# Other orders of work in an adaLN attention and quantised FFN kernel, with part of the FFN moved from VectorE to GpSimd

## The chip, the cores and the metric

The kernel runs on one core of one Trainium2 chip. The metric is device time in microseconds, the median of several executions; lower is better. Five engines work side by side and wait for each other by semaphores: TensorE (PE, with its weight loads as PEld), VectorE (DVE), ScalarE (ACT), GpSimd (POOL) and SyncE (SP), which here only issues DMAs. ScalarE issues the other DMAs.

## The reference, cut to what matters

`x` is (8, 256, 128). One layer is computed and added to `x`:

```python
# attention: 16 heads of 64, one shared key/value head, one extra "null" key
xn = ln(x, g_norm)
q = (xn @ Wq).reshape(b, n, 16, 64);  k, v = split(xn @ Wkv)
q = l2norm(q) * q_scale;  k = l2norm(k) * k_scale
sim = 8.0 * q @ k.T + attn_bias            # bias: a small MLP over relative positions
attn = softmax(causal(sim))
y = ln((attn @ v) @ Wout, g_out)
# FFN with fake quantisation to 8 bits; every scale is a maximum over the WHOLE tensor
xq = act_quant(y, clip_x)                  # scale = sigmoid(clip) * max|y| / 127
h = act_quant(silu(xq @ qw(w_gate).T) * (xq @ qw(w_up).T), clip_down)
return x + h @ qw(w_down).T
```

Two global maxima (of `y`, and of `h`) separate the kernel into stages: nothing of the FFN can start before the last `y`, and nothing can be rounded in the FFN's second half before the last `h`.

## The kernel before, in words

**Opening.** The relative-position MLP (`mlp_centre`, `mlp_silu`, `mlp_turn`), the keys of batch 0 (`k_norm2`, `k_normalise`, `kT_make`) and the first four "quarters" of q (`q_make_first`, `q_norm2`, `q_normalise`, `qT_make`, `qT_evac`) are made. A quarter is 128 rows by 8 heads. SP loads `b1b` and `g1b` (the MLP's second bias and gain) as its sixth and seventh DMA, lines 337 and 338.

**Loop.** `over_groups` runs every engine's `group(s)` over groups of four heads: `at` = 0 to 33, batch `s.b = at // 4`, `s.g = at % 4`. Each engine has its own hand-written order for a group; the engines are coupled by semaphores only. For a group, TensorE makes scores into two pairs of PSUM banks (front: heads 0 and 1, back: heads 2 and 3), the DVE adds the bias and takes row maxima (`score_pair`, L1227), ACT takes the exponent (`exponent`, L576), the DVE inverts the row sums (`invert`, L1235), POOL multiplies by the inverses (`normalise`, L443), TensorE transposes (`turn`, L917), ACT copies the result out (`pT_evac`, L586). One group later TensorE multiplies by the values (`values`, L874), the DVE copies that out (`oT_copy`, L1217) and TensorE multiplies by `Wout` (`y_products`, L829). The same loop carries the work of the next batches: x statistics (`x_stats`, `x_power`, `x_normalise`), keys (`kv_make`, `kv_evac`, `k_norm2`, `k_power`, `k_normalise`, `kT_make`) and one quarter of q per group (`q_make`, `q_square`, `q_norm2`, `q_power`, `q_normalise`). POOL's square roots are powers with exponent -0.5 (L396).

**Last groups.** Groups 32 and 33 hold no new scores (`s.live` is false). TensorE leaves them to `flush()`: it turns group 31's heads 0 and 1, multiplies the values of group 30, turns heads 2 and 3, and so on. Heads are turned only when ACT has emptied the pT buffer by reading order, since pT has one set of four tiles.

**FFN.** `ffn()` on TensorE; k counts 512-row blocks (4), f counts 128-wide tiles of the hidden width (IT = 3). ACT makes silu of the gate product (L662), the DVE multiplies it by the up product straight from PSUM (L1381). For f = 2 instead ACT copies both to SBUF (L671, L673) and POOL multiplies them (L474). The DVE takes one maximum per tile (`h_absmax`, L1360). After the second global maximum the DVE rounds to int8 (`h_quantise`, L1396), ACT widens to bf16 (L679), TensorE makes the down product, the DVE scales it (`down_scale`, L1400) and adds x (L1404, L1421), POOL adds x for block 1 (L477), SP stores.

## Time and profile before

| what | us |
|---|---|
| median of 3 executions | 302.04 (300.73 to 302.70) |
| the profiled execution | 302.66 |
| its span, first to last instruction | 300.9 |
| busy: PE, DVE, ACT, POOL | 259.3, 237.3, 228.0, 204.0 |

The profiled execution is 0.6 us above the median, and 1.8 us of it lie outside the span. Times in the rows below are microseconds from the start of the span. In a row of a timeline the first number is the start, the second the length, and "xN" merges N neighbouring instructions of one line. "idle before" is how long the engine had nothing to do and who ended that. In the loop a batch takes 29.05 us.

### The profile page before, as it was taken

To read this page: it belongs to the slowest core of one execution; us is meant where nothing else is said; L and a number is where in the kernel's file an instruction comes from. 1 tells how busy PE (TensorE), PEld (TensorE's weight loads), DVE (VectorE), ACT (ScalarE), POOL (GpSimd) and SP (SyncE) were. 2 spreads that over 40 slices of the span, in tenths; PEclk is the share of its full clock that TensorE was granted. 3 is DMA by queue.
4 is the path that set the end of the run, shared out by engine and by line. 5 is a ranking of instruction groups with operands and counts; after the bars stand their busy time and mean duration, and the time that the engine had idled before them with its cause. 6 is when DMAs were issued, how large, how long until landed. Compare 5 with 4: busy or idle time off the path is not lost.

```text
span 300.9 us, 7310 instructions
## 1 busy us (share of the span) xinstructions
PE 259.3 (86%) x2161; PEld 204.1 (68%) x2162; DVE 237.3 (79%) x965; ACT 228.0 (76%) x785; POOL 204.0 (68%) x394
## 2 busy tenths in 40 slices
PE   0769899989999999999999999999999987875260
PEld 0427778877787888778788878888787865761050
DVE  2758887887888888879887988787876767559993
ACT  1555989978987888888789978998888877249480
POOL 2277888788788779878987898778877755013301
PEclk9989999999999999999999999999999999899756
DMA  4279000000000000000000000000000020000013
GB/s 140 49 183 268 2 1 2 1 3 2 1 2 1 3 1 2 0 3 1 2 0 4 3 0 2 0 4 0 2 2 3 2 72 1 2 0 1 0 36 110
DMA packets 13083, 6.89 MB, mean 23 GB/s; under 512 B 1953, under 2 KB 12913, under 8 KB 13042
## 3 DMA queue, kind: packets, MB, share of 16 engines
q1 hardware_dynamic: 11874, 6.03, 7.5%
q10 hardware_dynamic: 1168, 0.36, 0.5%
q8 instruction: 20, 0.33, 0.5%
q14 instruction: 21, 0.17, 0.2%
HBM read 5.31 MB, written 1.07 MB: 21 GB/s over the span
## 4 chain that ended last, share of the span: by engine, by line
PE 63%; DVE 16%; POOL 5%; ACT 5%; issue 4%; DMA 3%; SPq 1%; POOLq 0%; DVEq 0%; ACTq 0%
PE bank L874 13%; PE bank L829 10%; PE front L855 7%; PE back L917 7%; PE front L917 5%; PE bank L718 5%; PE back L855 5%; PE bank L734 4%; DMA g1b<-in_L_cond_g_dram 3%; ACT prob L576 2%; DVE score L1227 2%; POOL prob L443 2%; DVE hmax L1360 2%; DVE oT L1217 2%; DVE oT L1396 2%
## 5 line engine op out<-in xcount | busy, mean ns | idle before, releaser
L576 ACT ACTIVATE prob<-score,negmax 128x258 f32<-128x258 f32 (+1 forms) x256 | 113.5, 450 | 30.5 <-DVE negmax L1227 30.5
L443 POOL TENSOR_SCALAR prob<-prob,rrow 128x258 f32<-128x258 f32 x254 | 107.3, 441 | 23.0 <-DVE rrow L1235 19.7
L396 POOL TENSOR_TENSOR rq<-qn,neghalf 128x8 f32<-128x8 f32 x32 | 53.3, 1666 | 2.7
L874 PE MATMUL bank<-pT,val 128*64 128x256 f32 (+1 forms) x512 | 49.7, 337 | 0.6 <-ACT pT L586 0.6
L576 ACT ACTIVATION_READ_ACCUMULATOR prob<-score,negmax 128x1 f32 x256 | 49.1, 192 | 0.0
L874 PEld LDWEIGHTS bank<-pT,val 128*64 128x64 f32 x512 | 32.2, 138 | 20.7 <-ACT pT L586 10.7
L829 PE MATMUL bank<-wout,oT 128*128 128x128 f32 x256 | 36.8, 287 | 5.4 <-DVE oT L1217 4.7
L1227 DVE CUSTOM_DVE_ANT_0 score<-back,bias 128x258 f32<-128x258 f32 (+1 forms) x128 | 38.0, 353 | 0.1
L1227 DVE CUSTOM_DVE_ANT_0 score<-front,bias 128x258 f32<-128x258 f32 (+1 forms) x128 | 37.8, 351 | 0.0
L829 PEld LDWEIGHTS bank<-wout,oT 128*128 128x128 f32 x256 | 31.0, 191 | 10.0 <-DVE oT L1217 6.9
L1096 DVE TENSOR_REDUCE qn<-sq 128x8 f32<-128x512 f32 x32 | 21.9, 685 | 19.6 <-ACT sq L522 19.0
L586 ACT COPY pT<-back 128x384 f32<-128x384 f32 x64 | 29.4, 480 | 4.7 <-PE back L917 3.4
L917 PE MATMUL back<-ident,prob 128*128 128x128 f32 x192 | 31.6, 285 | 0.1
L917 PE MATMUL front<-ident,prob 128*128 128x128 f32 x192 | 29.7, 273 | 1.1 <-POOL prob L443 1.1
L855 PE MATMUL front<-kT,qT 64*128 64x258 f32 (+1 forms) x256 | 29.7, 350 | 0.6 <-DVE qT L1107 0.2
L1217 DVE COPY oT<-bank 128x512 f32<-128x512 f32 x32 | 22.0, 688 | 9.0 <-PE bank L874 7.2
L586 ACT COPY pT<-front 128x384 f32<-128x384 f32 x64 | 26.7, 466 | 2.3 <-PE bank L874 2.3
L855 PEld LDWEIGHTS front<-kT,qT 64*128 64x128 f32 x256 | 22.2, 186 | 7.9 <-issue 5.4
L855 PE MATMUL back<-kT,qT 64*128 64x258 f32 (+1 forms) x256 | 26.9, 328 | 0.0
L917 PEld LDWEIGHTS back<-ident,prob 128*128 128x128 f32 x192 | 21.7, 144 | 5.1 <-DVE negmax L1227 3.4
L917 PEld LDWEIGHTS front<-ident,prob 128*128 128x128 f32 x192 | 22.8, 141 | 1.5 <-ACT pT L586 1.5
L855 PEld LDWEIGHTS back<-kT,qT 64*128 64x128 f32 x256 | 22.2, 187 | 2.2 <-issue 0.7
(199 smaller groups left out, 458.3 us busy)
## 6 DMA issues: line engine op xcount, KB each, us to landing
bias<-relative_table SPq DMA_DIRECT2D x8, 256.0 KB, 5.0
out_dram<-prob SPq DMA_DIRECT2D x4, 256.0 KB, 3.1
X<-in_x_dram SPq DMA_DIRECT2D x1, 896.0 KB, 13.3
prob<-in_L_cond_Wq_dram SPq DMA_DIRECT2D x1, 512.0 KB, 5.9
wout<-in_L_cond_Wout_dram SPq DMA_DIRECT2D x1, 512.0 KB, 14.5
prob<-in_L_ffn_w_down_dram SPq DMA_DIRECT2D x1, 176.0 KB, 2.4
X<-in_x_dram SPq DMA_DIRECT2D x1, 128.0 KB, 4.1
prob<-in_L_ffn_w_gate_dram SPq DMA_DIRECT2D x1, 128.0 KB, 2.1
```

Source lines behind the costliest of these rows:

```text
L396: pool.tensor_tensor(dst, src, neghalf[:, 0:width], ALU.pow).then_inc(done, 1)
L443: pool.tensor_scalar(prob[:, par, h, cols], prob[:, par, h, cols], rrow[:, par, h, t:t + 1], 1.0, ALU.mult, ALU.mult).then_inc(normed, 1)
L576: act.activation(prob[:, par, h, cols], score[:, h % 4, cols], ACT.Exp, scale=-1.0, bias=negmax[:, par, h, t:t + 1], accum_out=rowsum[:, p ...
L586: act.copy(pT[:, h % 4, :], bank[i][:, 0:3 * P]).then_inc(pT_ready, 1)
L718: last = pe.matmul(ps[:, :], xx[par][:, P * (q % 2):P * (q % 2) + P], ww[:, 512 * (q // 2):512 * (q // 2) + 512], start=xx is xTh and ww i ...
L829: pe.matmul(y_out(t), oT[:, m % 2, k, t * P:t * P + P], wout[:, k, :], start=k + t == 0, stop=False, skip_group_check=True)
L855: product = pe.matmul(banks[a][:, at:at + KEYS1 - c0], qT[par][rows, h // 2, t * P:t * P + P], kT[par][rows, c0:KEYS1], start=not masked, ...
L874: last = pe.matmul(ps[a * D:a * D + D, pair * N + i0:pair * N + N], val[m % 2][:, blk, :], pT[:, 2 * pair + a, c0:c1], start=blk == 1, sto ...
L917: product = pe.transpose(bank[i][:, k * P:k * P + P], prob[:, par, h, c0:c0 + P], ident[:, :])
L1096: dve.tensor_reduce(qn2[:, q, :], sq[:, :, :], AX.X, ALU.add).then_inc(q_n2, 1)
L1217: dve.tensor_copy(oT[:, m % 2, 2 * g:2 * g + 2, :].rearrange("p k n -> p (k n)"), (q_ps if at == GB * B - 1 else val_ps)[:, :])\
L1227: dve.tensor_tensor_reduce(score[:, h % 4, c0:c0 + w], ps[:, c0:c0 + w], bias[:, h, 0:w], -1.0, -3.0 * NEG, ALU.add, ALU.min, negmax[:, pa ...
```

## The change

1. **FFN.** `POOLED` names five (k, f) tiles instead of the four of f = 2: (0,2), (1,1), (1,2), (2,2), (3,2). The DVE makes seven products instead of eight. The twelve maxima become eight instructions, four of which cover two tiles. Block 0's addition of x goes from the DVE to POOL, and so does the multiplication that makes `sds`. All twelve `h_quantise` roundings come ahead of the first `down_scale`. The last maximum before the FFN takes one instruction less behind `yraw`.
2. **Loop.** On the DVE `invert` of the previous group's heads 2 and 3 moves behind the first `score_pair`, `k_normalise` moves from ahead of `oT_copy` to behind that `invert`, `k_norm2` goes ahead of `x_normalise`, `x_stats` one group earlier (g = 2). On POOL `x_power` moves from g = 0 of a batch, between two `normalise`, to g = 3 of the batch before, ahead of `q_power`. On ACT `kv_evac` goes between the two pairs of `pT_evac`.
3. **Last groups.** The loop ends at `LOOP = 30`; groups 30, 31 and the flush are written out in `ending()`. TensorE makes group 31's products in another order; group 30's turned heads are copied out by the DVE into a buffer of their own, `pTe`, so that ACT's copies of group 31 need not wait for `values(30)`; the weight preparation of the FFN (`ffn_weights`) is spread differently.
4. **Opening.** `b1b` and `g1b` are issued by ACT, ahead of `condk`, `qs` and `ks`. TensorE gets 40 idle transposes at the start and 3 in each `mlp_turn`, 6 more ahead of `qT_make(0)` and 6 ahead of the reading of the mask's minimum. `q_make_first(2)` goes ahead of the MLP's second layer. On the DVE the mask's minimum (L1142) moves from the start to behind `q_normalise(0)`, the table behind `k_normalise(0)`; `q_normalise(2)` goes between group 0's score pairs and `x_normalise(1)` behind them.

```diff
+POOLED = [(0, 2), (1, 1), (1, 2), (2, 2), (3, 2)]
+OWN = [(k, f) for k in range(4) for f in range(IT) if (k, f) not in POOLED]
+LOOP = GB * B - 2
...
 # POOL, group()
+                if s.g == 3 and s.b + 3 < B:
+                    x_power(s.b + 3)
                 if s.quarter is not None and s.quarter >= 4:
                     q_power(s.quarter, s.quarter % 4)
...
-                if s.g == 0 and s.prev is not None and s.b + 2 < B:
-                    x_power(s.b + 2)
...
+            def ending():
+                y_power(B - 2)
+                normalise(heads(LOOP - 1)[2:4])
+                for at in (LOOP, LOOP + 1):
+                    normalise(heads(at)[0:2])
+                    normalise(heads(at)[2:4] if at == LOOP else heads(at)[2:3])
+                y_power(B - 1)
...
 # PE
             pe.wait_ge(consts, 3)
+            keep_busy(40, qT_ps)
...
+            def ending(masked):
+                s = Group(LOOP)
+                first_scores(s, masked)
+                pe.wait_ge(pT_ready, GH * (LOOP - 1))
+                second_scores(s, masked)
+                values(LOOP - 2)
+                turn(s, 0)
+                turn(s, 1)
+                for pair in range(2):
+                    y_products(LOOP - 2, pair)
+                turn(s, 2)
+                turn(s, 3)
+                s = Group(LOOP + 1)
+                first_scores(s, masked)
+                pe.wait_ge(pT_ready, GH * LOOP)
+                second_scores(s, masked)
+                turn(s, 0)
+                turn(s, 1)
+                values(LOOP - 1)
+                turn(s, 2)
+                turn(s, 3)
+                for pair in range(2):
+                    y_products(LOOP - 1, pair)
+                s = Group(GB * B)
+                for i in range(4):
+                    turn(s, i)
+                pe.wait_ge(yT_ready, B - 1)
+                null_weights(s.null)
+                values(LOOP)
+                values(LOOP + 1)
+                for at in (LOOP, LOOP + 1):
+                    for pair in range(2):
+                        y_products(at, pair)
+                y_null(s.null)
...
 # DVE, group()
-                if s.kT is not None:
-                    k_normalise(s.kT)
...
                 if s.summed is not None:
                     oT_copy(s.summed)
                 if s.g == 2 and s.prev is not None:
                     y_normalise(s.prev)
-                if s.turned is not None and s.live:
+                if s.first:
+                    dve.wait_ge(ld_bias[s.g], 16 * 2)
+                score_pair(heads(s.at)[0:2])
+                if s.turned is not None:
                     invert(heads(s.turned)[2:4])
+                if s.kT is not None:
+                    k_normalise(s.kT)
+                if s.quarter >= 4:
+                    q_normalise(s.quarter, s.quarter % 4, q_ps)
+                if s.at == 0:
+                    q_normalise(2, 2, q_ps0[2])
+                score_pair(heads(s.at)[2:4])
+                if s.at == 0:
+                    x_normalise(1)
+                    qT_evac(2, 2, 0)
+                    q_normalise(3, 3, q_ps0[3])
+                invert(heads(s.at)[0:2])
...
 # DVE, the last groups
+            def pTe_copy(i):
+                dve.wait_ge(pT_done, heads(LOOP)[i][0] + 1)
+                dve.tensor_copy(pTe[:, i, :], bank[i][:, 0:3 * P]).then_inc(pTe_ready, 1)
...
 # DVE, FFN
+            h_product(0, 0)
+            h_product(0, 1)
+            h_absmax(0, 0, 0, 2)
+            h_product(1, 0)
+            h_absmax(1, 0, 2, 1)
+            h_absmax(2, 1, 0, 1)
+            h_product(2, 0)
+            h_product(2, 1)
+            h_absmax(3, 1, 1, 2)
+            h_absmax(4, 2, 0, 2)
+            h_product(3, 0)
+            h_product(3, 1)
+            h_absmax(5, 2, 2, 1)
+            h_absmax(6, 3, 0, 2)
+            h_absmax(7, 3, 2, 1)
...
+            for k in range(4):
+                h_quantise(k)
+            dve.wait_ge(sds_ready, 1)
+            for k in range(3):
+                down_scale(k)
```

## Rows read from the trace of the kernel before

**Rows 1.** Page: the span and its instructions.

```profile
span 300.9 us, 7310 instructions
```

**Rows 2.** Windows: length, then busy us of PE, PEld, DVE, ACT, POOL, then clock.

```profile
37.00:239.20 202.20, 197.95 (x1749) 161.82 (x1750) 168.08 (x742) 173.06 (x638) 165.36 (x319) 1.00 0.01 2
...
239.20:263.60 24.40, 21.05 (x175) 16.41 (x175) 15.70 (x66) 14.66 (x56) 9.88 (x25) 0.93 0.08 24
```

**Rows 3.** Waits, 38 to 239.3: us in total, times, longest.

```profile
PE bank L829 <- DVE oT L1217: 3.9, 6, 0.8
```

**Rows 4.** Timeline of POOL, DVE and PE, 116 to 122 (a group with g = 1).

```profile
116.89 1.80 POOL L443 TENSOR_SCALAR prob<-prob,rrow 128x258 f32<-128x258 f32 x4
...
119.09 0.72 POOL L396 TENSOR_TENSOR rk<-kn,neghalf 128x2 f32<-128x2 f32 x1
...
120.39 0.68 DVE L1217 COPY oT<-bank 128x512 f32<-128x512 f32 x1
...
121.12 1.16 PE L829 MATMUL bank<-wout,oT 128*128 128x128 f32 x8 [0.72 <-DVE oT L1217]
```

**Rows 5.** Timeline of DVE and POOL, 99 to 103 (a group with g = 2).

```profile
99.08 0.17 DVE L1235 RECIPROCAL rrow<-rowsum 128x4 f32<-128x4 f32 x1
...
99.16 0.40 DVE L1227 CUSTOM_DVE_ANT_0 score<-front,bias 128x258 f32<-128x258 f32 x1
...
100.11 1.66 POOL L443 TENSOR_SCALAR prob<-prob,rrow 128x258 f32<-128x258 f32 x4
...
100.25 0.69 DVE L1102 TENSOR_TENSOR qn<-bank,rq 128x512 f32<-128x512 f32 x1
...
102.35 1.66 POOL L443 TENSOR_SCALAR prob<-prob,rrow 128x258 f32<-128x258 f32 x4 [0.57 <-DVE rrow L1235]
```

**Rows 6.** Chain of waits of the opening: start, us, what.

```profile
3.43 10.39 DMA g1b<-in_L_cond_g_dram
...
37.05 0.94 PE bank L718 x3
```

**Rows 7.** Landing of ks, from its issue at 3.94.

```profile
L486 ACTq DMA_DIRECT2D ks<-in_L_cond_k_scale_dram x1: 453/453/453, 3.9 to 3.9; - x1
...
DMA to landing us min/median/max: 11.2/11.2/11.2
```

**Rows 8.** Timeline of DVE, group 0.

```profile
28.34 0.42 DVE L1227 CUSTOM_DVE_ANT_0 score<-front,bias 128x258 f32<-128x258 f32 x1
...
31.96 0.17 DVE L1235 RECIPROCAL rrow<-rowsum 128x4 f32<-128x4 f32 x1
```

**Rows 9.** Windows as in Rows 2, around two falls of the clock.

```profile
17.00:20.00 3.00, 1.04 (x4) 0.31 (x4) 1.25 (x5) 2.44 (x5) 2.54 (x3) 0.94 0.88 211
...
20.00:23.00 3.00, 2.85 (x8) 1.74 (x9) 1.20 (x3) 0.99 (x6) 2.07 (x3) 0.50 0.25 64
...
255.20:258.60 3.40, 3.40 (x23) 2.48 (x19) 1.23 (x3) 1.21 (x3) 0.11 (x1) 0.50 0.02 5
```

**Rows 10.** Chain of waits of the last groups.

```profile
254.79 2.50 PE bank L874 x16
...
257.29 1.45 PE back L917 x6
...
263.63 0.51 DVE ost L1241 x2
```

**Rows 11.** Timeline of DVE, ACT and POOL, FFN.

```profile
271.60 0.75 DVE L1381 SCALAR_TENSOR_TENSOR prob<-back,sgu,oT 128x512 f32<-128x512 f32 x1
...
273.62 1.28 ACT L662 ACTIVATE oT<-front,sgu 128x512 f32<-128x512 f32 x2
...
281.87 2.45 DVE L1360 TENSOR_REDUCE hmax<-prob 128x1 f32<-128x512 f32 x4
...
293.48 1.26 DVE L1404 TENSOR_TENSOR prob<-prob,X 128x512 f32<-128x512 f32 x1
...
295.57 0.69 DVE L1421 TENSOR_TENSOR prob<-prob,X 128x512 f32<-128x512 f32 x1
```

More of the change, by code:

```diff
@@ L97, in held @@
     eng.sem_inc(passed, 1)
+LOOP = GB * B - 2
 def over_groups(group):
-    for at in range(GB * B + 2):
+    for at in range(LOOP):
         group(Group(at))
@@ L206, in build @@
         ymax = sb("ymax", [P, B])
+        gabs = sb("gabs", [P, 1])
         yraw = sb("yraw", [P, 1])
@@ L336, in _ @@
             sp.dma_start(mask_u[:, :], mask.rearrange("(a b) n -> a (b n)", a=1)).then_inc(ld_mask, 16)
-            for dst, src in ((b1b[:, :], row(b1)), (g1b[:, :], row(g1))):
-                sp.dma_start(dst, src).then_inc(ld_mlp, 16)
             for dst, src in ((w2s[:, :], w2), (b2c[:, :], col(b2))):
@@ L484, in _ @@
             act.dma_start(w1s[:, :], w1).then_inc(ld_w1, 16)
+            for dst, src in ((b1b[:, :], row(b1)), (g1b[:, :], row(g1))):
+                act.dma_start(dst, src).then_inc(ld_mlp, 16)
             for dst, src in ((condk[:, :], row(cond[0])), (qs[:, :], row(q_scale)), (ks[:, :], row(k_scale))):
@@ L542, in _ @@
             mlp_turned(0)
+            kv_evac(0, halves(misc))
+            q_square(0, q_ps0[0])
+            q_square(1, q_ps0[1])
+            mlp_silu(1)
+            mlp_turned(1)
+            q_square(2, q_ps0[2])
+            act.wait_ge(kT_done, 1)
+            for par in range(2):
+                act.copy(kT[par][:, 0:KEYS1:P + 1], misc[:, 2 * P:2 * P + 2]).then_inc(null_a, 1)
+            kT_evac(0, halves(misc))
+            v_copy(0)
+            act.activation(table_load[:, 1:2], neghalf[:, 0:1], ACT.Exp)
+            q_square(3, q_ps0[3])
+            act.wait_ge(wq_ready, 1)
+            act.copy(wqh[:, :], wq[:, :]).then_inc(wq_high, 1)
             act.wait_ge(ld_mask, 16)
@@ L616, in group @@
                     pT_evac(s.turned, 1)
-                if s.at == GB * B - 1:
-                    exponent(heads(s.at)[3])
+                if s.kv is not None:
+                    kv_evac(s.kv, front_tails)
                 if s.turned is not None:
@@ L623, in group @@
                     null_evac(s.null)
-                if s.kv is not None:
-                    kv_evac(s.kv, front_tails)
                 if s.kT is not None:
@@ L735, in qT_make, with keep_busy @@
                 last.then_inc(qT_done, 1)
+            def keep_busy(count, ps):
+                for _ in range(count):
+                    pe.transpose(ps[:, 0:P], ident[:, :], ident[:, :])
             def mlp_turn(layer):
@@ L742, in mlp_turn @@
                 last.then_inc(mlp_t, 1)
+                keep_busy(3, qT_ps)
                 pe.wait_ge(mlp_a, 2 * layer + 2)
-            def keep_busy(count, ps):
-                for _ in range(count):
-                    pe.transpose(ps[:, 0:P], ident[:, :], ident[:, :])
             pe.wait_ge(consts, 3)
+            keep_busy(40, qT_ps)
             for t in range(2):
@@ L867, in values @@
                 last_group = at == GB * B - 1
+                turned = pTe if at == LOOP else pT
                 ps = q_ps if last_group else val_ps
@@ L874, in values @@
                             last = pe.matmul(ps[a * D:a * D + D, pair * N + i0:pair * N + N], val[m % 2][:, blk, :],
-                                             pT[:, 2 * pair + a, c0:c1], start=blk == 1, stop=blk == 0,
+                                             turned[:, 2 * pair + a, c0:c1], start=blk == 1, stop=blk == 0,
                                              skip_group_check=True)
@@ L1179, in _ @@
             q_norm2(3, 3)
-            q_normalise(2, 2, q_ps0[2])
-            x_normalise(1)
             def ffn_weights(h):
@@ L1274, in group @@
             def group(s):
-                if s.quarter is not None and s.quarter >= 4:
+                if s.quarter >= 4:
                     q_norm2(s.quarter, s.quarter % 4)
-                if s.kT is not None:
-                    k_normalise(s.kT)
-                if s.turned == GB * B - 1:
-                    invert(heads(s.turned)[2:4])
-                    last_normalise()
                 if s.summed is not None:
```

286 lines of the change are left out of this document (142 added, 144 removed).

## The prediction, made blind

> **What bounds the kernel now.** I read the page first, for the span of 300.9 us [rows 1], then the windows by stage. The reader is to see there that the loop is TensorE's: from 37 to 239.2 it is busy 197.95 of 202.2 us at full clock, while the next engine, ACT, has 173.06 [rows 2]. So a change of order in the loop can give back about 4 us at most, which is what PE lacks. The waits say where those are: 3.9 us in six waits of `y_products` on the copy `oT` [rows 3], one in each g = 1 group of batches 1 to 6. The last groups are another thing: 24.4 us, in which PE is busy 21.05 us, part of it at half clock [rows 2]. The FFN's first half is the DVE's, without a gap worth naming between 271.60 and 284.3 [rows 11]. The opening hangs on a DMA and then on a chain that goes through all engines [rows 6].
>
> **Loop, the wait that goes.** In g = 1 POOL normalises from 116.89 to 118.69, then makes `rk` until 119.81; the DVE scales the keys after it and only then copies `oT`, from 120.39; `y_products` starts at 121.12, 0.72 us late [rows 4]. Afterwards `oT_copy` comes first, and stands behind nothing but `values`, which ends near 118.9. With 0.7 us for the copy [rows 4] it is there by 119.7, before PE has made its scores (it would ask at 120.4). `x_power` is gone from ahead of that `normalise`, so the keys are scaled near 121.5, behind the first score pair, and are wanted at about 121.8. All six waits go: -3.9 us. If the keys come late, the wait returns there, at the 0.3 us or so that I have misjudged. `kv_evac` fills a pause of ACT before the back pair is turned; `x_stats` and `x_power` in their new places fill pauses of over 1 us that their engines had while q was squared. I count these at nothing; without the pause each costs its own length of up to 1 us, once a batch.
>
> **Loop, the wait that comes.** `invert` of heads 2 and 3 now stands behind four score halves. In g = 2 it ran at 99.08, the halves took 99.16 to 100.25, that is 1.09 us, and POOL began with those heads at 100.11, as soon as it was free [rows 5]. POOL starts 0.38 us after an `invert` starts (101.97 to 102.35, the release in the last line of [rows 5]). The new `invert` starts at 100.17, so POOL starts at 100.55, 0.44 late, and ends at 102.21 instead of 101.77 (1.66 us for four instructions [rows 5]). Head 3 is turned today once its scores are taken from PSUM, at 102.05, so 0.16 us of the 0.44 shows. Six batches: +1.0 us. In the other groups POOL is held by the powers of q until after the new `invert`. Loop: -2.9 us, bounds -3.9 (the lag hides) and -1.2 (all of 0.44 shows in six groups).
>
> **Last groups.** Today this stage is a zigzag: values of group 30 wait for ACT's last exponents and copies, and PE idles and falls to half clock. The values at 254.79 take 2.50 us for 16 products against the loop's 1.45, the turns at 257.29 take 1.45 against 0.66 [rows 10]; the clock row beside them is 0.50 [rows 9]. That excess is 1.05 + 0.8 = 1.85 us. At full clock PE's work here is 21.05 - 1.85 = 19.2 us. In the new order I walked through the queues from 239.2 on. Three waits remain on PE: 0.75 us ahead of `y_products(28)`, because the DVE takes two score pairs (2 x 1.09 us [rows 5]) before `oT` and `yn`; 0.7 us ahead of `y_products(29)`, whose copy (0.68 [rows 4]) stands behind two `pTe` copies; 0.5 us for POOL's head 2 of group 31. So y is complete at 239.2 + 19.2 + 1.95 = 260.35 by busy times. Walking by starting times, which overlap less in the count, gives 259.1. Today it is 263.63 [rows 10]. That is -3.3 to -4.5; I take -4.0. Behind it `gabs`, one maximum and the joined end lie beside POOL's power of about 1.2 us; one small DVE instruction goes from the path, -0.25 us.
>
> **FFN, first half.** The DVE goes from 8 to 7 products (0.66 us apart), -0.66 us; a maximum costs 0.6 (2.45 us for four [rows 11]), of which about 0.06 is not streaming, and four joined pairs save 0.25. From this the DVE would need 11.6 instead of 12.7 us. But each tile given to POOL costs ACT two passes instead of one. ACT's passes are 0.58 us apart (two of them end 1.15 us after 273.62 [rows 11]). After 273.62 ACT has one pass for (1,0), two for (1,1), the widening of xq (0.51), two for (1,2), then (2,0), which starts at 273.62 + 5 x 0.575 + 0.51 = 277.0. The DVE product follows a gate by 0.74 us, so at 277.7; the DVE has by then done its three products and maxima up to block 1 and is idle since 276.4. That wait of 1.3 us, with 0.4 us of smaller ones for (1,0) and (0,2), more than eats the 0.9 us. From 277.7 on: 4 products, 2.64, 7 tiles of maxima, 3.9 with joins, and the gap to the end gives 285.0 with the last reduction, against 284.3: +0.7 us. Bounds: -0.9, if ACT does not hold it, and +1.0.
>
> **FFN, second half.** With all roundings first ACT loses its wait of 0.3 us, but the third down product waits for `down_scale(0)`, which comes after twelve roundings. The DVE's last addition starts at 295.57 [rows 11]; I come to 295.5. I take -0.05, bounds -0.6 and +0.4. In the row of 293.48 the addition takes 1.26 us, against 0.69 for the same shape at 295.57 [rows 11], and POOL's addition runs beside it. The Trainium skill (SBUF — State Buffer, section "SBUF: two separate sides") says that the DVE and GpSimd share one pair of ports under an exclusive lock, and the loser waits. By that rule two additions on POOL would hold the DVE's until the second ends, and the last addition would start at 295.65, which moves the sum by 0.1.
>
> **Opening.** `g1b` lands 10.39 us after its issue, at 13.82 [rows 6]. Ahead of three loads on ACT's queue it should land near 11.5, so the MLP's second layer starts at about 12, 1.9 us sooner. But the `ks` load moves behind it. It lands at 15.1 today [rows 7], when nobody waits; now the DVE will stand at it from about 13.3, and every power on POOL is queued behind. I take 15.5 for it (bounds 14 and 17.5). From there the chain of powers and q quarters brings the first scores of group 0 to the DVE at 25.6 if TensorE is at full clock, at 26.7 if it is at half, against 28.34 [rows 8]. Then the order in group 0 takes some back. From first score to `invert` it is 3.62 us today (28.34 to 31.96 [rows 8]); with `q_normalise(2)` between the pairs, and `x_normalise(1)` behind them, for which PE's x transposes and so its q transposes wait, I add up 5.5 us. `q_make(4)` is due at 36.9 (half) or 35.8 (full) instead of 37.05 [rows 6]: -0.15 or -1.2 us. I take -0.7, bounds +1.3 (ks at 17.5) and -2.0. The 40 transposes lie ahead of the first x and cover nothing; at the slow spacing they would end at 10 and cost up to 0.3.
>
> The clock decides between those two. Its row is 0.50 for 20 to 23, after a stretch of 3 us in which PE worked 1.04 us [rows 9], and the new opening leaves PE about as sparse there. By the Trainium skill (TensorE: Matmul & The Clock Gate, "What's actually happening") the low rate is the default and comes back after an idle window. By that rule alone the opening, which has no long idle stretch, would keep full clock and give -1.2; the row shows that a stretch that is not idle was enough for the fall.
>
> **Sum.** -0.7 - 2.9 - 4.0 - 0.25 + 0.7 - 0.05 = -7.2 us. The profiled execution took 302.66 and becomes 295.5; it stands 0.6 above the median, so from 302.04 I get 294.8.
>
> **Rivals.** *The fall of the clock stays in the last groups*: PE still has 1.95 us of waits there, and one fall costs the 1.85 us above: 296.7. *The FFN is not held by ACT*: -0.9 instead of +0.7: 293.2. *Keys late*: ks at 17.5 or later, opening +1.3 instead of -0.7: 296.8. *Full clock from the transposes on*, the skill's rule named above: 294.3. *The cuts of waits do nothing*, as POOL's and DVE's chain through q bounds a group at the same 7.0 us anyway and the six waits only move to the turns: loop 0, 297.7. *The other side*: the later `invert` puts POOL on the path in every one of 29 groups. Each then loses the 0.44 us, 12.8 us in place of the 1.0 that I count: 306.6. Against it: in g = 0 and 3 POOL is bound by the powers of q, which end after the new `invert`. It would decide from 0.25 us a group on (7.2 / 29).
>
> **How the numbers follow.** Forecast 0.45, clock rival 0.15, FFN rival 0.1, keys 0.1, full clock 0.06, waits only moved 0.1, POOL in every group 0.04. The range takes in all but the last, with the bounds that add up at the low side: 291.0 to 299.0. About 1% is what a measurement of this kernel can tell from no change, so faster means below 299.0: 0.89. Within 1%: 0.07, where two of the rivals fall together. Slower: 0.04.
>
> **What would show it.** Right: no wait of `y_products` on `oT` in the loop and a batch of about 28.5 us instead of 29.05; a wait of some 0.15 us more in the turn of head 3 in g = 2; 19 to 21 us from the scores of group 30 to `y_stats(7)` with the clock at 1.00; a DVE gap of about 1.3 us ahead of product (2,0); in the opening a DVE wait for the `ks` load. Wrong: gaps of PE in front of each turn of head 2 (POOL in every group); a first `invert` after 33; a clock row of 0.50 in the last groups.

## The result, and the profile after

| | before | changed |
|---|---|---|
| median of 20 executions each, us | 301.84 (299.51 to 304.01) | 302.61 (301.04 to 305.75) |
| the profiled execution, us | 302.66 | 301.27 |

The ratio on record is 1.0055, 95% interval 1.0031 to 1.0079: no gain at all, where 294.8 us and a gain of 7 us had been forecast. (It isn't the quotient of the two medians, which is 1.0026; the loss is 0.8 us by the medians and 1.7 by the ratio.) Six of the changed kernel's 20 executions, two of them counted as slow and left out of the ratio, took 304.3 to 305.8 us at a mean granted clock of 0.946 to 0.948, where the others have 0.959 to 0.975; none of them was traced, so what happens there stays open. The changed kernel's profiled execution lies 1.3 us below its own median, that of before 0.8 us above its own, so the pair of traces shows a span 1.5 us shorter where the medians show 0.8 us longer. The traces are used here for where the time goes inside, and the medians for what a version is worth.

The page of the changed kernel, its span:

```profile
span 299.4 us, 7421 instructions
```

I put the same events of the two traces side by side (start times from the timelines, us) and subtracted from one mark to the next. "Forecast" is the term of the prediction's sum:

```
event                                    before   changed  later by   stage: measured  forecast
q_make(4), PE                             37.05    39.97    +2.92     opening  +2.92    -0.7
front scores of group 30, PE             239.21   242.44    +3.23     loop     +0.31    -2.9
y_stats(7), DVE                          263.63   262.96    -0.67     last gr. -3.90    -4.0
first product of the FFN, DVE            271.60   270.73    -0.87              -0.20    -0.25
second global maximum (amax), DVE        284.36   284.23    -0.13     FFN 1    +0.74    +0.7
last addition of x, DVE                  295.57   295.18    -0.39     FFN 2    -0.26    -0.05
end of the span                          300.85   299.40    -1.45     store    -1.06     none
```

Four terms came out close to the forecast; two, the opening and the loop, are wrong by 3.6 and 3.2 us, together 6.8 of the forecast gain of 7.2. The last line isn't an effect of the change: from the last addition to the end took 5.28 us in before, 4.22 here, and between 4.17 and 5.58 in the other kernels below, all with the same last store.

**Loop.** Windows: length, then busy us of PE, PEld, DVE, ACT, POOL, then clock. The same stretch, from the first scores of group 2 to those of group 30, of the changed kernel and then of before; the last row is the changed kernel's last groups, to be read against [rows 2]:

```profile
40.84:242.44 201.60, 197.45 (x1747) 161.31 (x1747) 166.66 (x736) 175.67 (x634) 165.18 (x316) 1.00 0.01 2
```

```profile
37.91:239.21 201.30, 197.08 (x1747) 161.35 (x1747) 167.32 (x736) 172.16 (x635) 164.46 (x317) 1.00 0.01 2
```

```profile
242.40:262.90 20.50, 18.77 (x175) 15.33 (x176) 16.66 (x69) 13.19 (x52) 9.78 (x25) 1.00 0.11 28
```

TensorE lacks 4.15 us in the changed loop and 4.22 in the old one. So its waits haven't gone, although the waits of [rows 3] have: the waits of PE in the changed loop, 40 to 242.4 us, in total, times and longest, are these, and none is on `oT`:

```profile
PE back L964 <- POOL prob L452: 1.7, 6, 0.3
PE front L738 <- DVE kz L1150: 0.6, 1, 0.6
PE back L857 <- POOL prob L452: 0.5, 2, 0.3
PE bank L755 <- issue: 0.5, 1, 0.5
PE bank L773 <- DVE qn L1167: 0.4, 1, 0.4
```

The time itself shows the rest of the account. The lag behind before at the front scores of a group, us:

```
group   2     3     4     5     6     7     8     9     10    11   ...  26    27    28    29    30
lag   +2.92 +3.45 +4.29 +4.58 +3.84 +4.09 +4.10 +4.13 +3.48 +3.73 ... +2.58 +2.82 +3.04 +3.23 +3.23
```

Each batch gains 0.64 to 0.74 us where the wait on `oT` stood (group 5 to 6, 9 to 10 and so on; only 0.14 in batch 6), 3.4 us in all. Each then loses 0.25 between g = 2 and g = 3. But ahead of that, between group 2 and group 5, stands a loss of 1.66 us that comes once, and that no step of the prediction had.

**The g = 2 group.** Timeline of the DVE, POOL and PE, 101 to 106 us: start, length, engine, line, and in brackets the idle time ahead and who ended it.

```profile
103.68 0.17 DVE L1298 RECIPROCAL rrow<-rowsum 128x4 f32<-128x4 f32 x1
...
104.07 3.07 POOL L452 TENSOR_SCALAR prob<-prob,rrow 128x258 f32<-128x258 f32 x7 [0.44 <-DVE rrow L1298]
...
105.88 0.52 PE L964 MATMUL back<-ident,prob 128*128 128x128 f32 x3 [0.29 <-POOL prob L452]
```

`invert` stands behind the first score pair, POOL is idle 0.44 us until it comes, and the turn of head 3 is 0.29 us late. The 0.44 is the number of the prediction to the digit; what PE sees of it was put at 0.16.

**The start of the loop.** Timeline of PE, DVE and POOL, 43 to 55 us (groups 2 and 3, batch 0):

```profile
43.26 0.69 DVE L1280 COPY oT<-bank 128x512 f32<-128x512 f32 x1 [1.00 <-PE bank L921]
...
45.07 0.58 DVE L1150 SCALAR_TENSOR_TENSOR kz<-kv,rk,qks 128x128 f32<-128x128 f32 x2
...
53.26 0.69 DVE L1167 TENSOR_TENSOR qn<-bank,rq 128x512 f32<-128x512 f32 x1 [0.80 <-POOL rq L409]
```

```profile
45.80 0.30 PE L738 MATMUL front<-ident,kz 128*128 128x128 f32 x1 [0.64 <-DVE kz L1150]
...
54.01 0.66 PE L773 MATMUL bank<-ident,qn 128*128 128x128 f32 x4 [0.39 <-DVE qn L1167]
```

```profile
50.43 0.71 POOL L409 TENSOR_TENSOR rstd<-mv,neghalf 128x2 f32<-128x2 f32 x1
```

The keys of batch 1 are scaled one group later than in the other batches (`late` is 1 in batch 0). At 42.26 the DVE had nothing to do for 1.00 us, which is where `k_normalise` stood; now it runs at 45.07, behind a score pair, and TensorE waits 0.64 us for it. One group on, `x_power(3)` (50.43, with its short instruction at 50.16) is ahead of `q_power`, so q is scaled at 53.26 after 0.80 us of idle DVE, and TensorE waits 0.39. These two waits, and one of 0.26 us on POOL at 62.54 (the first of L857), are 1.3 us of the 1.66; no wait of TensorE in the trace names the rest.

**Opening.** Timeline of ACT, 4.8 to 12.4 us:

```profile
4.84 0.45 ACTq L509 DMA_DIRECT2D ks<-in_L_cond_k_scale_dram  x1
5.33 5.61 ACTq L511 DMA_DIRECT2D vcol<-in_cond_dram  x2
...
12.37 0.68 ACT L552 ACTIVATE prob<-prob,mrs 128x128 f32<-128x128 f32 x2
```

ACT issues eleven loads now. The first nine take 0.45 to 0.68 us each, the last two together 5.61 us (1.21 and 4.37 by the chain of waits), and in that time ACT does nothing else: its first silu starts at 12.37 instead of 9.03. TensorE stands still for the last 3.79 us of the way there, and the granted clock falls behind that, from 14.1 to 17.5 us, and is at 1.00 from there into the FFN:

```profile
13.10 0.44 PE L785 MATMUL front<-ident,prob 128*128 128x128 f32 x2 [3.79 <-ACT prob L552]
```

The chain of waits that ends in the first score goes through the MLP's second layer, which comes behind the keys (its silu at 19.63), and through two instructions that the change had moved there, the table and the mask's minimum:

```profile
21.90 0.47 DVE table L1234
...
22.97 0.79 DVE mask_min L1237
```

Then the DVE in group 0 (timeline, 29 to 35 us), against [rows 8]:

```profile
29.08 0.43 DVE L1290 CUSTOM_DVE_ANT_0 score<-front,bias 128x258 f32<-128x258 f32 x1 [1.15 <-PE front L898]
...
30.20 0.69 DVE L1167 TENSOR_TENSOR qn<-bank,rq 128x512 f32<-128x512 f32 x1
...
31.92 0.85 DVE L1133 TENSOR_SCALAR xn<-X,mv,rstd 128x128 f32<-128x128 f32 x2
...
34.94 0.17 DVE L1298 RECIPROCAL rrow<-rowsum 128x4 f32<-128x4 f32 x1
```

and the wait of PE that belongs to it, in the waits of 28.5 to 40 us:

```profile
PE bank L724 <- DVE xn L1133: 2.8, 1, 2.8
```

TensorE stands 2.8 us in front of the transposes of `xn`, which the DVE makes only behind both score pairs of group 0. From first score to first `invert` it is 5.86 us, against 3.62. The first `invert` is at 34.94; the prediction had named one after 33 as a sign that it is wrong.

**Last groups and FFN.** The waits of PE, 242.4 to 263 us:

```profile
PE bank L872 <- DVE yn L1313: 1.1, 1, 1.1
PE back L964 <- POOL prob L452: 0.4, 1, 0.4
PE bank L747 <- DVE negmax L1290: 0.2, 1, 0.2
```

1.7 us of waits remain, and the clock is 1.00 throughout. That holds beyond this trace: the two traces with the old last groups have the fall of the clock in them and take 24.4 us from the front scores of group 30 to `y_stats(7)`, the eleven with the new ones have no fall there and take 20.5. In the FFN (timeline of ACT and the DVE, 274 to 285 us) the wait that was forecast is there:

```profile
276.13 1.32 ACT L702 ACTIVATE oT<-front,sgu 128x512 f32<-128x512 f32 x2
```

```profile
274.26 1.28 DVE L1452 TENSOR_REDUCE hmax<-prob 128x1 f32<-128x512 f32 x2
276.90 0.75 DVE L1470 SCALAR_TENSOR_TENSOR prob<-back,sgu,oT 128x512 f32<-128x512 f32 x1 [1.36 <-ACT oT L702]
```

### The profile page after: what moved, and what is told of

It is laid out like the page before. It is cut to its first block, busy times and chain, and to the rows that moved or that the text cites. A ratio compares the mean times of both kernels' runs of the same rounds, so it can differ in the third digit from the quotient of the medians.

```text
span 299.4 us, 7421 instructions
## 1 busy us (share of the span) xinstructions
PE 264.1 (88%) x2219; PEld 211.4 (71%) x2220; DVE 235.9 (79%) x963; ACT 229.9 (77%) x782; POOL 207.4 (69%) x397
## 4 chain that ended last, share of the span: by engine, by line
PE 60%; DVE 20%; POOL 7%; issue 6%; ACTq 3%; ACT 3%; DVEq 0%; POOLq 0%
PE bank L921 14%; PE front L898 7%; PE bank L872 7%; PE back L964 7%; PE bank L755 6%; POOL prob L452 5%; DVE score L1290 5%; PE back L898 4%; PE front L964 4%; PE bank L773 3%; DVE oT L1280 2%; ACTq L511 2%; DVE oT L1495 2%; DVE hmax L1452 2%; DVE yn L1313 1%
## 5 line engine op out<-in xcount | busy, mean ns | idle before, releaser
L599 ACT ACTIVATE prob<-score,negmax 128x258 f32<-128x258 f32 (+1 forms) x256 | 113.4, 450 | 16.4 <-DVE negmax L1290 16.4
L921 PE MATMUL bank<-pT,val 128*64 128x256 f32 x496 | 47.1, 332 | 0.0
L921 PEld LDWEIGHTS bank<-pT,val 128*64 128x64 f32 x496 | 30.8, 136 | 19.3 <-ACT pT L609 9.9
L609 ACT COPY pT<-back 128x384 f32<-128x384 f32 x62 | 28.7, 482 | 9.0 <-PE back L964 8.6
L964 PE MATMUL back<-ident,prob 128*128 128x128 f32 x192 | 30.2, 277 | 2.8 <-POOL prob L452 2.1
L898 PE MATMUL back<-kT,qT 64*128 64x258 f32 (+1 forms) x256 | 26.7, 326 | 0.0
```

The source lines that it names most:

```text
L599: act.activation(prob[:, par, h, cols], score[:, h % 4, cols], ACT.Exp, scale=-1.0, bias=negmax[:, par, h, t:t + 1], accum_out=rowsum[:, p ...
L609: act.copy(pT[:, h % 4, :], bank[i][:, 0:3 * P]).then_inc(pT_ready, 1)
L898: product = pe.matmul(banks[a][:, at:at + KEYS1 - c0], qT[par][rows, h // 2, t * P:t * P + P], kT[par][rows, c0:KEYS1], start=not masked, ...
L921: last = pe.matmul(ps[a * D:a * D + D, pair * N + i0:pair * N + N], val[m % 2][:, blk, :], turned[:, 2 * pair + a, c0:c1], start=blk == 1, ...
L964: product = pe.transpose(bank[i][:, k * P:k * P + P], prob[:, par, h, c0:c0 + P], ident[:, :])
```

## The experiments

Each version was timed with runs of the kernel before beside it, whose median was 301.20 us in the first four, 301.77 in the next four and 301.94 in the last three; it was 301.84 beside the changed kernel. Where two versions of different rounds are compared, the difference is taken of their distances to these medians, and the plain one is given too. "Stage" below is the difference between two of the marks of the table above.

**Theory:** the opening loses because ACT is held at its queue, because `x_normalise(1)` stands behind group 0's scores, and because `ks` is late; the loop loses because of the first batch and of `invert` in g = 2. **Main rival:** one cause only. If ACT's hold were all, its removal would give the opening back; if the order in group 0 were all, the hold would cost nothing.

### The vcol loads on SyncE

```diff
 # ACT
-            for dst, src in ((vcol[0:D, :], ...), (vcol[D:P, :], ...)):
-                act.dma_start(dst, src).then_inc(ld_v, 16)
 # SP, behind wout
+            for dst, src in ((vcol[0:D, :], ...), (vcol[D:P, :], ...)):
+                sp.dma_start(dst, src).then_inc(ld_v, 16)
```

> The changed kernel, but the two vcol loads are issued by SP behind wout instead of by ACT as its tenth and eleventh load. Theory 1 (ACT stood 4.4 us at the issue of its last load, and the MLP started 3.3 us late for that): ACT's first silu comes back to about 9 us from 12.37, the first scores of group 0 reach the DVE at 26 to 27 instead of 29.08, and group 1's first scores start about 2 us earlier than in the changed kernel (33.6). Time about 2 us below the changed kernel. Rival (the ks load and POOL's powers bound the opening anyway): silu early, but first scores still at 28.5 or later, time unchanged.

Measured: 303.59 us, ratio 1.0083 (1.0043 to 1.0123). The hold is gone, the silu starts at 8.97 instead of 12.37, and nothing is gained: the first score comes at 29.27, and the median is 2.4 us above that of before beside it, against 0.8 for the changed kernel. Timeline of the DVE in this kernel, 17 us:

```profile
17.22 0.23 DVE L1223 CUSTOM_DVE_ANT_0 ksq<-condk 128x64 f32<-128x64 f32 x1 [3.68 <-DMA ks<-in_L_cond_k_scale_dram]
```

The DVE stands 3.68 us at the load of `ks`. In the changed kernel it arrives at the same instruction at 17.30, when `ks` has landed (16.94). So up to this instruction the hold was hidden behind the late `ks`, to within 0.1 us. Behind it the two traces are not alike. TensorE has nothing to do for 5.16 us here; the clock is at 0.50 from 16.6 to 23.5 us (and again from 33.7 to 37.1), while the changed kernel has 1.00 from 17.5 on; and the idle transposes of the change (`keep_busy`, L780) stand in the chain of waits with 3.07 us. Timeline of PE, then three pieces of the chain:

```profile
19.51 0.69 PE L785 MATMUL front<-ident,prob 128*128 128x128 f32 x2 [5.16 <-ACT prob L552]
```

```profile
20.20 0.64 PE bank L780 x3
...
22.64 1.12 PE bank L780 x6
...
25.06 1.31 PE bank L780 x12
```

The run shows that taking the hold away alone brings nothing. It doesn't show that the hold is free at equal clock, and whether the chain would be shorter without these 21 transposes, of which 15 are the change's, was not run.

### x_normalise(1) back ahead of group 0's scores

```diff
             q_norm2(3, 3)
+            x_normalise(1)
...
                 if s.at == 0:
-                    x_normalise(1)
                     qT_evac(2, 2, 0)
```

> The changed kernel, but x_normalise(1) stands ahead of group 0's first score pair again, as before the change. Theory 1 (PE's x and q transposes wait for it): PE's wait of 2.75 us ahead of xT_make(1) goes, group 1's first scores start 1.5 to 2 us earlier than 33.6, the time falls by about 1.5 us. Rival (ACT's exponents bound group 0 and 1): the wait moves to the first invert, and group 2's first scores stay at 40.8.

Measured: 300.39 us, ratio 0.9950 (0.9915 to 0.9985). From first score to `invert` 4.04 us instead of 5.86; the wait of 2.8 us is gone; the lag at group 2 falls from 2.92 to 1.28 us. One moved pair of instructions is worth 1.6 us in the trace, and 1.6 in the medians as well (0.8 above before turns into 0.8 below; 2.2 from median to median).

### Both

The two edits above together.

> The changed kernel with both edits: vcol on SP and x_normalise(1) ahead of group 0's scores. If the two causes are independent, group 2's first scores start at about 37 (40.84 changed, 37.91 before) and the time is 3.5 to 4 us below the changed kernel, so about 299 against 301.8 before. If they share one bound, the gain is no more than the larger one, about 2 us.

Measured: 300.58 us, ratio 0.9962 (0.9932 to 0.9993), as with the second edit alone: again nothing is gained by taking away the hold. The trace is like that of the first run, with TensorE idle for 5.52 us, the clock at 0.50 from 18.4 to 25.2 us, and 3.23 us of idle transposes in the chain of waits.

### The opening of before

The changed kernel with the orders and loads of the old opening.

> The changed kernel with the whole opening as before (loads, idle transposes, orders of ACT, PE and DVE up to and in group 0), loop, last groups and FFN as changed. Theory 1: group 2's first scores start at 37.9 as before the change, the later transient of groups 2 to 5 and the rest stay, so the time is 2.9 us below the changed kernel. Rival (the opening's loss would be made up later in the loop, as POOL's and DVE's chain sets the pace): group 10 starts at the same time as in the changed kernel, 101.2, and the time is unchanged.

Measured: 299.83 us, ratio 0.9938 (0.9902 to 0.9974). The whole new opening costs 2.1 us by the medians (0.8 above before turns into 1.4 below; 2.8 from median to median), and 2.4 in the traces, where the lag at group 2 falls from 2.92 to 0.48. The lag rises from 0.48 at group 2 to 2.10 at group 5: the loss of 1.62 us at the loop's start is there with the old opening as well, so it belongs to the loop.

### The new last groups alone

The kernel before, with `ending()`, `LOOP` and the maximum that takes one instruction less behind `yraw`.

> The kernel before with the new last groups alone (opening, loop and FFN as before). Theory: the last groups were worth 3.9 us in the changed kernel and depend on nothing else that changed, so y_stats(7) starts 3.9 us earlier than in before (263.6 to 259.8) with no fall of the clock behind 240 us, and one DVE instruction less brings 0.2 more: 297.1 us beside 301.2. Rival: a good part of the 3.9 us came from the state in which the new loop leaves the engines, or the clock falls again: 299 us or more.

Measured: 298.43 us, ratio 0.9885 (0.9835 to 0.9936). Stage from the scores of group 30 to `y_stats(7)`: 3.9 us shorter than before, with no fall of the clock there. The median gains 3.3 us of the 4.1 that the stages show; the interval (296.8 to 299.8) holds both.

### The new FFN alone

> The kernel before with the new FFN alone (five tiles on GpSimd, joined maxima, all roundings first, two additions on GpSimd). Theory: the first half loses 0.74 us to the wait of the product (2,0) for ScalarE, the second gains 0.26: 301.7 us beside 301.2, with a VectorE gap of 1.4 us ahead of that product. Rival: the wait was due to the stages before, and the first half gains 0.9: 300.1 us.

Measured: 301.70 us, ratio 0.9994 (0.9963 to 1.0025). First half +0.73 us, second half -0.27. The wait for ACT has nothing to do with the stages before.

### The keys' loads on SyncE, ahead of x

On top of both opening edits:

```diff
 # SP, behind nb and ahead of the large load of x
+            for dst, src in ((condk[:, :], ...), (qs[:, :], ...), (ks[:, :], ...)):
+                sp.dma_start(dst, src).then_inc(ld_keys, 16)
             sp.dma_start(X[:, 2:, :], x_dram[:, 2:, :]).then_inc(ld_x, 16)
 # ACT: condk, qs, ks go, the two vcol loads come back
```

> The kernel with both opening edits (x_normalise(1) first, ScalarE's queue not full), and now condk, qs and ks issued by SyncE ahead of the large load of x, the two vcol loads back on ScalarE. Theory: in the last two runs with an early silu the chain hung on the landing of ks at 17.2 and 17.5; ahead of the load of x it lands near 14, and the first score comes at 26.5 instead of 29.9: 297.4 us. Rival: ks is late for the sake of the DMA engines, not of the queue, or TensorE runs at half clock in the gap: first score 28.5 or later, 299.5 us or more.

Measured: 298.17 us, ratio 0.9890 (0.9851 to 0.9929). Timeline of the DVE:

```profile
16.06 0.23 DVE L1223 CUSTOM_DVE_ANT_0 ksq<-condk 128x64 f32<-128x64 f32 x1 [1.35 <-DMA ks<-in_L_cond_k_scale_dram]
...
26.71 0.43 DVE L1291 CUSTOM_DVE_ANT_0 score<-front,bias 128x258 f32<-128x258 f32 x1 [0.15 <-DMA bias<-relative_table]
```

`ks` lands at 16.0 instead of 17.5: 1.5 us earlier, not the 3.5 that I expected of the queue's order. It takes 10.7 us from its issue in the new place and 12.1 in the changed kernel, so most of its lateness isn't the order on ACT's queue. The first score is 3.2 us earlier than in the kernel with both edits. 1.5 us of that is `ks`; the remaining 1.7 goes with the clock, which in the trace of that kernel is at 0.50 from 18.4 to 25.2 us and here at 1.00 from 14.5 us on. An early `ks` with ACT's hold left in place was not run. Now the load of the bias is what ends last.

### The loop repaired

On top of the old opening:

```diff
+                if s.kT is not None and s.first:
+                    k_normalise(s.kT)
                 if s.summed is not None:
                     oT_copy(s.summed)
...
+                if s.g == 2:
+                    invert(heads(s.turned)[2:4])
                 score_pair(heads(s.at)[0:2])
-                if s.turned is not None:
+                if s.turned is not None and s.g != 2:
                     invert(heads(s.turned)[2:4])
...
-                if s.g == 2 and s.b + 3 < B:
+                if s.g == (3 if s.first else 2) and s.b + 3 < B:
                     x_stats(s.b + 3)
 # POOL: x_power(3) back to group 4
```

> The changed kernel with the opening of before, and two repairs of the loop: in batch 0 k_normalise(1) is ahead of oT_copy, x_stats(3) and x_power(3) where they were before; in every g = 2 group invert of heads 2 and 3 is ahead of the first score pair again. Theory: the start-up loss of 1.6 us between group 2 and group 5 goes, and so does the 0.25 us a batch of g = 2 (1.5 us): 296.8 us beside 299.8 without the repairs. Rival for the first: the start-up loss comes from the kernel's state at that point and stays, 298.3 us. Rival for the second: PE's wait moves to the score copies behind the invert, and a batch stays as long as it was, also 298.3 us.

Measured: 296.22 us, ratio 0.9817 (0.9789 to 0.9845), 3.6 us below the same kernel without the two repairs (4.2 by the distances to before; the loop in the two traces is 2.7 us shorter, 198.75 against 201.47). Groups 2 to 5 take 22.78 us (before 22.73, changed 24.38), and g = 2 to g = 3 loses nothing in later batches. The waits of PE from 38 to 237 us, all of them:

```profile
PE back L851 <- POOL prob L454: 0.3, 1, 0.3
```

```profile
38.38:237.13 198.75, 197.52 (x1748) 161.29 (x1747) 166.93 (x736) 175.40 (x634) 163.98 (x316) 1.00 0.01 2
```

The loop takes 198.75 us, 2.55 less than before. Both rivals fall. The edit moves `k_normalise`, `x_stats` with `x_power`, and `invert` at once, so how the 1.66 us of the start divide between them isn't shown.

### Four tiles on GpSimd, joined maxima

```diff
-POOLED = [(0, 2), (1, 1), (1, 2), (2, 2), (3, 2)]
+POOLED = [(0, 2), (1, 2), (2, 2), (3, 2)]
...
             h_product(1, 0)
-            h_absmax(1, 0, 2, 1)
-            h_absmax(2, 1, 0, 1)
+            h_product(1, 1)
+            h_absmax(1, 0, 2, 1)
+            h_absmax(2, 1, 0, 2)
...
-            h_absmax(3, 1, 1, 2)
+            h_absmax(3, 1, 2, 1)
```

> The kernel with the opening of before and the repaired loop, with four tiles on GpSimd in the FFN as before (f = 2 of every block), but joined maxima and all roundings first. Theory: the fifth tile is what costs, as ScalarE needs two passes for it; the first half then takes 12.5 us from the first product to the second maximum instead of 13.5 (before 12.76), the second half keeps its gain of 0.26 us: 295.2 us beside 296.2 with five tiles. Rival: the joined maxima themselves cost (they wait for the later of two products) and the first half stays at 13.3 or more: 296.0 us.

Measured: 294.88 us, ratio 0.9753 (0.9706 to 0.9800). Timeline of the DVE, 269 to 278 us:

```profile
270.82 0.74 DVE L1467 SCALAR_TENSOR_TENSOR prob<-back,sgu,oT 128x512 f32<-128x512 f32 x1
...
277.60 0.16 DVE L1487 TENSOR_REDUCE amax<-hmax 128x1 f32<-128x8 f32 x1
```

No idle time ahead of any product, first half 12.58 us (five tiles 13.50, before 12.76). The joined maxima gave 0.18 us where 0.25 was forecast; the fifth tile cost 0.92.

### All that helped, together

> All that helped together: the new opening with x_normalise(1) first and the condk, qs and ks loads on SyncE, the repaired loop, the new last groups, four pooled tiles with joined maxima. Theory: the gains add, 298.2 - 1.6 (start-up) - 1.5 (g = 2) - 1.0 (FFN) = 294.1 us, with TensorE at full clock to the first scores. Rival: with the first scores 3 us earlier the loads of the bias (they ended last ahead of the first score in the run with the keys on SyncE) or the transient of batch 0 take back what the repair of the loop gave: 295.7 us.

Measured: 294.72 us, ratio 0.9761 (0.9713 to 0.9809). The better opening shows in the trace (q, scores and `y_stats(7)` all 1.5 us earlier than in the kernel before this one) but not in the medians of six and four executions. Whether it is worth anything in this combination stays open.

### Without the 40 idle transposes

> The kernel with all together, without the 40 idle transposes that TensorE makes ahead of its first transpose of x. Theory: they lie in a stretch in which TensorE waits for x anyway and cost nothing, and they keep the granted clock at 1.00 until the keys are made; without them a row of 0.50 appears before 20 us and the first score comes about 1 us later: 295.1 us. Rival: they make no difference to the clock, 294.1 us.

Measured: 293.53 us, ratio 0.9742 (0.9694 to 0.9789), against 0.9761 with them: no difference that these runs can tell. My theory of them falls all the same: no row of 0.50 appears before 20 us without them, and the first score comes 0.95 us earlier, at 25.72. The windows of the kernel with the transposes, and then of the one without (columns as above):

```profile
16.00:19.00 3.00, 1.61 (x10) 0.94 (x11) 1.66 (x5) 2.05 (x5) 2.83 (x5) 1.00 1.04 260
19.10:22.50 3.40, 3.40 (x14) 2.67 (x13) 3.40 (x6) 2.18 (x6) 2.27 (x4) 0.50 0.19 50
```

```profile
16.00:19.00 3.00, 1.85 (x10) 0.90 (x10) 1.62 (x5) 2.05 (x5) 2.83 (x5) 1.00 1.08 272
19.10:22.50 3.40, 3.37 (x25) 2.60 (x24) 3.40 (x6) 2.94 (x8) 2.27 (x4) 1.00 0.18 37
```

```profile
12.79 1.91 PE L725 MATMUL bank<-prob 128*128 128x512 f32 x2
...
20.82 1.92 PE L725 MATMUL back<-prob 128*128 128x512 f32 x2
```

```profile
11.88 1.02 PE L764 MATMUL bank<-prob 128*128 128x512 f32 x2
```

TensorE is then done sooner and idle for longer ahead of the second turn of the MLP, 2.65 us against 1.01 without the transposes, and the clock falls 1.8 us after that pause. Early speed bought nothing here, since the next input wasn't there.

This last kernel is the best of the study, 2.6% below before and about 3% below the changed kernel.

## Why the prediction was wrong, and where it was right

**Opening: the step that failed is the sum -0.7 (measured +2.92, outside its bounds of -2.0 to +1.3).** Three things.

- *`ks` at 15.5.* It landed at 16.94, inside the bounds that I gave it (14 to 17.5). The DVE went on at 17.30, 1.8 us behind the 15.5. The walk then put the first score 11.2 us behind `ks` at half clock and 10.1 at full; it was 11.8, although the clock was at 1.00 from 17.5 on. So 1.7 us are missing in the walk itself: it had the MLP's second layer start at about 12, but the DVE begins it at 15.20 and its silu runs at 19.63, so that this silu, the table and the mask's minimum stand between the keys and the first score. Together the first score is at 29.08, not 25.6 or 26.7. The rival "keys late" had this mechanism with its place, but priced it at 2.0 us against the forecast and hence at +1.3 for the opening. That is 1.6 us short of what was measured.
- *The order in group 0.* I added up 5.5 us from first score to `invert`; it is 5.86. The step was right, and it was the one to act on: the second run shows 1.6 us for one moved pair. I counted the late `x_normalise` but trusted the early keys to pay for it.
- *ACT's issues.* I counted each DMA moved onto ACT's queue at its landing, and not at what the issue does to ACT. The hold of 4.37 us wasn't foreseen. In the first and third runs its removal brought nothing: `ks` was late as well, the MLP's second silu came only 0.85 us sooner in the first (18.78), and behind it TensorE worked at half clock with idle transposes on the chain. What the hold costs at equal clock isn't shown. It also took away the premise of the two clock cases, an opening without a long idle stretch: TensorE was idle for 3.79 us.

**Loop: -2.9 forecast, +0.31 measured, outside its bounds of -3.9 to -1.2.** The wait on `oT` went in all six groups, as forecast; but the batches gained 3.4 us by it, not 3.9. The late `invert` cost 0.25 us a batch, not 0.16: of POOL's 0.44 us, 0.29 shows at the turn of head 3, which I had put later than it is. That is 1.5 us over the six, not 1.0. The step that failed outright is the sentence that counts `k_normalise`, `x_stats` and `x_power` in their new places at nothing. It was argued from the timeline of steady batches. Batch 0 has another shape: its keys are one group late, two batches of x are prepared in neighbouring groups, and there the new orders cost 1.66 us. A steady batch takes 28.69 us, where 28.5 had been forecast. The run with the loop repaired shows both causes: with the orders put right the loop gives -2.55, near the forecast. About 0.6 us of small losses (0.03 a group in most batches, 0.2 a group in groups 27 to 29) I can't assign.

**Last groups: -4.0 forecast, -3.90 measured.** The method held: PE's busy time at full clock plus the waits that a walk through the queues finds. Of the three waits one was larger (1.1 instead of 0.75, on `yn`), one as forecast (0.4 for 0.5), and one didn't come (0.7 on the copy of group 29). The clock didn't fall, and the rival of a fall at that place is refuted.

**One instruction less behind `yraw`: -0.25, measured -0.20.**

**FFN, first half: +0.7 forecast, +0.74 measured.** The gate of (2,0) was to start at 277.0 in the time of before, 276.13 once the 0.87 us of shift are taken off: it started at 276.13, and the DVE waited 1.36 us for it. A rival said that ACT would not hold the FFN; the sixth and ninth runs refute it. **Second half: -0.05 forecast, -0.26 measured**, inside its bounds. Here the port rule was weighed. Timeline of POOL and the DVE of the changed kernel:

```profile
291.30 2.50 POOL L497 TENSOR_TENSOR prob<-prob,X 128x512 f32<-128x512 f32 x2 [5.31 <-DVE prob L1499]
```

```profile
292.84 0.69 DVE L1499 TENSOR_TENSOR prob<-bank,sds 128x512 f32<-128x512 f32 x1 [1.02 <-PE bank L1096]
293.56 0.79 DVE L1508 TENSOR_TENSOR prob<-prob,X 128x512 f32<-128x512 f32 x1
```

The DVE's addition starts at 293.56, 0.24 us before POOL's end by the profile, and takes 0.79 us, 0.10 more than the same shape undisturbed in [rows 11]. The Trainium skill (SBUF — State Buffer, section "SBUF: two separate sides") says that of a DVE instruction with two SBUF inputs and a GpSimd instruction the later one blocks until the other ends. By that rule the addition should take 0.24 + 0.69 = 0.93 us here; 0.79 shows some delay but not all of it, and POOL's span is too rough to settle it.

**The rival on the other side** (POOL on the path in every group) didn't come: only g = 2 groups show it, 1.7 us in six. The result ended on that side anyway, by two mechanisms that I had priced too low or not at all. The chance of 0.89 for a gain rested on terms that I had treated as bounded on one side by zero. The range was also narrower than its own terms: their bounds add up to 289.9 and 300.0 us, not 291.0 and 299.0, and the measured 302.6 lies outside both.

## What to carry to other kernels

An edit in a loop with a pipelined start has two prices, one for the steady iterations and one for the first: walk the first iterations' queues as well, for they have fewer covers and other neighbours. When a chain has two late inputs, taking away one shows nothing; read which one the next consumer would wait for before you count a gain. Read the clock of both traces, too, before you say that a change brought nothing: here the run without the hold was at half clock where the other was at full. Filler instructions for the clock are work like any other once the clock has fallen. And handing a second engine one more tile has to be costed on the engine that feeds it: here the DVE saved 0.66 us and waited 1.36 for ACT.

## What the runs showed of the hardware

**The engine that issues a DMA can be held by it.** Nine loads on ACT's queue cost 0.45 to 0.68 us each, the tenth 1.21 and the eleventh 4.37, until 10.94 us. ACT computed nothing in that time. With the same two loads on SyncE, ACT had issued its last load by about 5.3 us and started its first silu 3.4 us earlier.

**The same instructions, with the clock falling or not.** The opening of the kernel before was run unchanged in the version with the new FFN alone. There the row of 20 to 23 us has the clock at 1.00, where [rows 9] have 0.50 for the same stretch:

```profile
17.00:20.00 3.00, 1.10 (x7) 0.55 (x7) 1.81 (x6) 2.36 (x4) 1.98 (x3) 1.00 0.90 214
20.00:23.00 3.00, 2.92 (x15) 1.60 (x14) 2.00 (x5) 1.88 (x7) 2.46 (x5) 1.00 0.30 79
```

TensorE had been busy 1.10 us of the 3 ahead, against 1.04. The first score came at 26.57 instead of 28.34 us. Of these 1.77 us 0.56 were there before the fall, as `g1b` landed 9.84 us after its issue and not 10.39; 1.2 go with the fall. The other traces with the old opening agree: from the DVE's first instruction for the keys to the first score it is 11.4 us without a fall in this one, and 12.6 to 13.3 in the five with one. In the changed kernel the fall is at another place, and the stretch ahead of it has 0.77 us of work in 3:

```profile
11.00:14.00 3.00, 0.77 (x5) 0.53 (x5) 0.00 (x0) 2.94 (x7) 0.00 (x0) 1.00 0.64 162
14.10:17.50 3.40, 3.40 (x10) 2.38 (x11) 2.20 (x14) 0.37 (x1) 0.90 (x2) 0.50 0.92 240
```

The Trainium skill (TensorE: Matmul & The Clock Gate, "What's actually happening") calls the low rate the default, which comes back after an idle window. The changed kernel agrees: the 0.77 us lie behind an idle stretch of 3.79 us, and the clock falls 1.0 us after it. So do the first and third runs, idle for 5.16 and 5.52 us. The kernel before doesn't fit as well: from 16.4 us to its fall at 19.65 the pauses are 0.81, 0.46 and 0.94 us, and pauses of 1.03, 0.46 and 1.44 us at the same places brought no fall in the other execution. A prediction for a kernel with such a sparse opening has to carry 1 to 2 us of scatter that no edit explains; the executions of the kernel before, unchanged, spread from 299.5 to 304.3 us.
